# Convolution, mixer, attention and experts in one kernel: fewer dummy matmuls, expert biases in two row groups, last residuals on VectorE, a bank apart for the variance

## The chip, the cores and the metric

The kernel runs on one core of one Trainium2 chip. The metric is device time in microseconds (us). Engines: TensorE (PE, its weight loads PEld), VectorE (DVE), ScalarE (ACT), GpSimd (POOL) and SyncE (SP), which issues the transfers. TensorE writes into PSUM, which has eight banks.

## What is computed

The input x is 8 images of 32 channels and 16 x 16 pixels. Cut to what matters here:

```python
# a 1x1 layer, a depthwise 3x3 convolution, silu, a two-way state-space mixer, batch norm, a gate:
x = gated_mixer(x)                                   # g * x + x
t = tokens(x)                                        # 8 x 256 tokens x 32
t = t + attention(layernorm(t))                      # causal
h = layernorm(t)
p = softmax(h @ router_w + router_b)                 # 8 experts
top_p, top_i = top_k(p, 2); top_p /= top_p.sum(-1)
out = einsum("bnd,edc->bnec", h, expert_w) + expert_b
t = t + sum over the two chosen experts of top_p * out
```

## The kernel before

All of it stays on chip. The 8 images are two halves (bh = 0 and 1) of four images each; a half is a tile of 128 partitions (four images times 32 channels) by 256 pixels. Pixels go in blocks of 128, so there are four output blocks, k = 0 to 3, and blocks 0 and 1 belong to half 0. Each engine has a program written out by hand, and runs it in that order; semaphores join the engines. Nothing is scheduled by a planner.

An fp32 matmul stands in the trace as two pieces, a bf16 one as one. So `x16` at L587 is eight matmuls.

- Start, L571 to L607: `keep_warm(8)`, eight matmuls on a tile of zeros whose result nobody reads (L569, bf16, 512 columns each), then the 1x1 layer (L576) as soon as the pack `pa` and x are loaded; ScalarE copies it out (L352); the folding of weights (L580), four taps of the convolution for each half (L587) while VectorE does the other five (L1066) and adds both (L1073); ScalarE's silu (L361), then its load of another function table (L363) and an exponential (L365). TensorE folds three more weights (L594, L596), runs `keep_warm(5)`, and then the step sizes (L605), which wait for silu. VectorE (L1095, L1097) and ScalarE (L389, L391) turn them into decays, on which all of the mixer rests.
- End of the mixer, L778 to L802: groups 0 to 7 of the state-space scan; `outputs(i)` multiplies a group's matrix with its values (L721) and, for the second group of a unit, adds the carried state (L727). `states` (L709) makes that state, ScalarE copies it (L433). `mean_squares(u)` (L734) feeds the norm on ScalarE (`rms`, L454 and L456). The last group's output goes through VectorE (`gated`, L1156), ScalarE's square (L429), `mean_squares(3)` and the norm before the last `mixer_out` (L792).
- Second norm, router and experts, L1010 to L1033: for each half `centre2` (L915), ScalarE's square (L513), `variance2` (L920), ScalarE's root (L517, L519), VectorE's scaled tile h2 (L1267), the router: first the bias (`route_bias`, L927, one row of contraction), then the weights (`route`, L933), into `router_bank[bh]`, which `variance2` has used before. VectorE's selection of two experts is a chain of some fifteen small instructions (L1277 to L1345). `experts(j)` (L947) is one image's product with all 8 experts, in the 32 rows of the array that hold this image; images 4 to 7 wait until VectorE has weighed images 0 to 3 (`weighted`, L1354, `mix_ready`). `keep_warm` stands at L1012, L1019, L1025 and L1029, the last with 12 matmuls.
- End, L1034 to L1043: for each output block `mixed_head(k)` starts the sum in PSUM with the residual (`t2` times the identity, L968) and adds the expert biases (`wtt`, the turned weights, L971); `mixed(k)` adds the eight weighed products (L982, for the last block four, as VectorE sums the halves, L1408). ScalarE copies each block out (`store_copy`, L536) and SP stores it (L275). `weights_turned(bh)` (L955) and ScalarE's `w_copy` (L531) make `wtt`. Blocks take turns in two banks, `mixed_bank`.

Of the kernel before, what the change touches and what calls it, by code (L numbers as in the profile page):

```python
# [28 lines left out]
ALU = mybir.AluOpType  # L29
ACT = mybir.ActivationFunctionType  # L30
# [44 lines left out]
def program(nc, x_in, pa_in, pb_in, pc_in, pd_in, out):  # L75
    ctx = ExitStack()
    with ctx:
# [163 lines left out]
        wt_bank = [bank[5], bank[5]]  # L241
# [4 lines left out]
        router_bank = [bank[5], bank[0]]  # L246
        mixed_bank = [bank[4], bank[0]]
# [96 lines left out]
        def _(act):  # L344
# [170 lines left out]
            def ln2_root(bh):  # L515
                act.wait_ge(S["var2_done"], bh + 1)
                act.activation(l2[:, bh, :], router_bank[bh][:, 0:L], ACT.Ln, bias=eps[:, :]).then_inc(S["l2_ready"], 1)  # L517
# [16 lines left out]
            def store_copy(k):  # L534
                act.wait_ge(S["mixed"], k + 1)
                act.activation(fin[:, k * Q:(k + 1) * Q], mixed_bank[k % 2][:, 0:Q], ACT.Copy)\  # L536
                   .then_inc(S["fin_ready"], 1)
# [21 lines left out]
            store_copy(2)  # L559
            store_copy(3)  # L560
# [3 lines left out]
        def _(pe):  # L564
# [7 lines left out]
            keep_warm(8, 7)  # L572
# [25 lines left out]
            keep_warm(5, 7)  # L598
# [114 lines left out]
            def outputs(i):  # L713
# [4 lines left out]
                y = [unit[i // 2][C * q:C * q + C, Q * (k % NC):Q * (k % NC) + Q] for q in range(BQ)]  # L718
                for q in range(BQ):
                    m = mmat[:, i, q, :]  # L720
                    mm = pe.matmul(y[q], s1t[:, d, k, q, :], m if d == 0 else back(m), start=False, stop=(step == 0))  # L721
                if step == 1:
                    pe.wait_ge(S["h_copied"], BH * d + bh + 1)
                    pe.wait_ge(S["cpfx_ready"], d + 1)
                    for q in range(BQ):
                        r = slice(C * q, C * q + DI)
                        mm = pe.matmul(y[q], hst[r, d, bh, :], cpfx[r, d, bh, :], start=False, stop=True)  # L727
                mm.then_inc(S["y_done"], 1)

# [49 lines left out]
            skipped(6)  # L779
            outputs(6)  # L780
            skipped(7)
            states(1, 1)
            mean_squares(2)
            outputs(7)
# [132 lines left out]
            def variance2(bh):  # L917

                pe.wait_ge(S["c2sq_ready"], bh + 1)
                pe.matmul(router_bank[bh][:, 0:L], packs["mean32"], c2sq[:, bh, :], start=True, stop=True)\  # L920
# [30 lines left out]
            def weights_turned(bh):  # L951
                pe.wait_ge(S["w_ready"], bh + 1)
                if bh:
                    pe.wait_ge(S["wt_copied"], 1)
# [3 lines left out]
            def mixed_head(k):  # L958

                bh = k // NC  # L960
                o = mixed_bank[k % 2][:, 0:Q]
                pe.wait_ge(S["t2_ready"], bh + 1)
                pe.wait_ge(S["cen2_ready"], 2)
# [565 lines left out]
```

## Time and profile before

| | us |
|---|---|
| median of 3 runs | 93.61 |
| lowest and highest | 93.31, 93.78 |
| the profiled execution | 94.22 |
| its span in the profile | 92.4 |
| around the span | 1.8 |
| TensorE busy | 82.9 |
| VectorE busy | 57.9 |
| ScalarE busy | 40.7 |

The trace is of one execution; starts are counted from the beginning of its span. The chain of waits goes back from the last instruction: at each step to what released it. Its rows give the time by which each step carries the end forward, which for pipelined matmuls is less than what one of them lasts. The timeline gives each group of instructions from its first start to its last end.

### The profile page before, as it was taken

Reading aid. Unit: us, or ns where it says so; the run is one execution under the profiler, and the core shown is the slowest. Engines: PE = TensorE matmul, PEld = TensorE weight load, DVE = VectorE, ACT = ScalarE, POOL = GpSimd, SP = SyncE. Lnnn points to the kernel's source line nnn. Section 1 sums busy time; section 2 is a strip of 40 time slices with the busy share of each in tenths; the row PEclk is TensorE's granted clock in tenths of the full one; section 3 lists DMA queues with packets and bytes.
Section 4 is the critical chain, followed back from the end, with each engine's and each line's share of the span. In section 5 each row is a group of like instructions: output and inputs, shape, how many; then the busy total and the mean of one; then the engine's idle time right before and its main releaser. Section 6 shows DMA issues by size and latency. Waiting matters only on the chain.

```text
span 92.4 us, 1937 instructions
## 1 busy us (share of the span) xinstructions
PE 82.9 (90%) x740; PEld 54.2 (59%) x744; DVE 57.9 (63%) x149; ACT 40.7 (44%) x93; POOL 20.2 (22%) x31
## 2 busy tenths in 40 slices
PE   4999999994999999896589799999999989999890
PEld 1458774553666564445344676767474555789780
DVE  1329968999989999641543359177129789894000
ACT  4031277979739512354379741714660521011011
POOL 6050005967899009800000000000000000000000
DMA  2993000000000000000000000000000000000001
GB/s 32 402 366 146 0 0 0 0 0 0 0 11 0 7 0 0 0 7 0 0 0 4 0 0 7 0 0 0 0 7 0 0 0 0 0 11 28 28 0 57
DMA packets 1305, 2.57 MB, mean 28 GB/s; under 512 B 144, under 2 KB 784, under 8 KB 1296
## 3 DMA queue, kind: packets, MB, share of 16 engines
q1 hardware_dynamic: 1152, 2.31, 6.9%
q10 hardware_dynamic: 144, 0.14, 0.4%
q8 instruction: 6, 0.10, 0.4%
q14 instruction: 3, 0.02, 0.1%
HBM read 2.19 MB, written 0.26 MB: 26 GB/s over the span
## 4 chain that ended last, share of the span: by engine, by line
PE 67%; DVE 15%; ACT 10%; issue 5%; DVEq 0%; ACTq 0%
PE banks L569 8%; PE banks L982 7%; DVE lmat L1135 5%; PE banks L947 4%; PE banks L587 4%; DVE pre L1128 4%; PE banks L669 3%; PE banks L904 3%; PE banks L734 3%; PE banks L686 2%; PE banks L971 2%; PE banks L576 2%; ACT data L503 2%; PE banks L872 2%; PE banks L721 2%
## 5 line engine op out<-in xcount | busy, mean ns | idle before, releaser
L569 PE MATMUL banks<-warm 128*128 128x512 bf16 x40 | 11.8, 429 | 1.4 <-DVE warm L1048 1.2
L1135 DVE TENSOR_TENSOR_SCAN lmat<-banks,data 128x512 f32<-128x512 f32 x8 | 9.8, 1220 | 0.8 <-PE banks L669 0.7
L569 PEld LDWEIGHTS banks<-warm 128*128 128x128 bf16 x44 | 4.4, 108 | 6.1 <-issue 2.0
L982 PE MATMUL banks<-pa,lmat 128*128 128x128 f32 x56 | 6.9, 279 | 0.2 <-issue 0.2
L982 PEld LDWEIGHTS banks<-pa,lmat 128*128 128x128 f32 x56 | 6.6, 192 | 0.3
L297 POOL TENSOR_TENSOR data<-pa,dt_dir 128x512 f32<-128x512 f32 x4 | 4.0, 1039 | 8.7 <-DVE dt_dir L1111 8.7
L1354 DVE TENSOR_TENSOR lmat<-banks,wtok 128x256 f32<-128x256 f32 (+1 forms) x12 | 5.5, 503 | 0.2
L536 ACT ACTIVATE fin<-banks 128x128 f32<-128x128 f32 x4 | 1.1, 278 | 9.9 <-PE banks L982 9.9
L1141 DVE TENSOR_TENSOR mmat<-banks,lmat 128x512 f32<-128x512 f32 x8 | 5.3, 669 | 0.0
L503 ACT ACTIVATE data<-banks 128x384 f32<-128x384 f32 x8 | 3.4, 492 | 3.0 <-PE banks L888 2.9
L297 POOL TENSOR_TENSOR data<-pb,dt_dir 128x512 f32<-128x512 f32 x4 | 4.1, 1042 | 0.0
L947 PE MATMUL banks<-pd,h 32*128 32x256 f32 x32 | 4.1, 399 | 0.0
L686 PE MATMUL banks<-s 16*128 16x128 f32 x64 | 4.0, 321 | 0.0
L454 ACT ACTIVATE yln<-banks,eps 128x256 f32<-128x256 f32 x4 | 1.9, 473 | 4.4 <-PE banks L734 4.4
L1241 DVE TENSOR_REDUCE nmax<-banks 128x2 f32<-128x256 f32 x4 | 1.7, 420 | 3.4 <-PE banks L860 3.4
L669 PE MATMUL banks<-pa,da 128*128 128x128 f32 x16 | 2.5, 278 | 1.5 <-DVE lmat L1135 1.5
L587 PE MATMUL banks<-o1p,diag 128*128 128x256 f32 x16 | 3.7, 385 | 0.0
L624 PE MATMUL banks<-o,fold_w 128*128 128x512 f32 x8 | 3.6, 592 | 0.0
L314 POOL TENSOR_TENSOR pre<-tap,pre 128x510 f32<-128x510 f32 (+2 forms) x3 | 3.4, 1149 | 0.4 <-ACT tap L384 0.2
L686 PEld LDWEIGHTS banks<-s 16*128 16x128 f32 x64 | 2.5, 182 | 1.6 <-issue 1.6
L306 POOL TENSOR_TENSOR wbx<-s1t,lmat 128x128 f32<-128x128 f32 x4 | 2.1, 533 | 5.9 <-DVE lmat L1135 4.4
L721 PE MATMUL banks<-mmat,s1t 128*32 128x128 f32 x64 | 3.4, 285 | 0.0
(200 smaller groups left out, 184.3 us busy)
## 6 DMA issues: line engine op xcount, KB each, us to landing
pc<-in_pc SPq DMA_DIRECT2D x1, 962.5 KB, 7.1
pb<-in_pb SPq DMA_DIRECT2D x1, 446.0 KB, 3.8
pd<-in_pd SPq DMA_DIRECT2D x1, 336.0 KB, 7.5
x<-in_x SPq DMA_DIRECT2D x1, 256.0 KB, 3.0
out<-fin SPq DMA_DIRECT2D x4, 64.0 KB, 1.6
pa<-in_pa ACTq DMA_DIRECT2D x1, 133.5 KB, 3.2
```

The lines of the kernel that those rows point to most:

```text
L297: pool.tensor_tensor(data1[:, i, :, :], one.rearrange("p (o t) -> p o t", o=1).to_broadcast([P, BQ, Q]), spread(dt_dir[:, d, BQ * k:BQ * k ...
L503: act.activation(probt[:, b, :], bank[ST_BANK[b]][:, 0:384], ACT.Exp).then_inc(S["prob_ready"], 1)
L569: pe.matmul(bank[scratch][:, :], warm[:, 0:P], warm[:, :], start=True, stop=True)
L587: mm = pe.matmul(conv_bank[bh][:, 0:L], diag[:, t, :], o1p[:, bh, t // 3:t // 3 + H, t % 3:t % 3 + W], start=(i == 0), stop=(i == len(PE_T ...
L669: mm = pe.transpose(dab_bank[:, Q * q:Q * q + Q], da[:, col:col + 1].to_broadcast([P, P]), packs["ident"] if d == 0 else packs["rev"])
L686: mm = pe.matmul(g_ps[:, q, :], s1[r, d, bh, at], c if d == 0 else back(c), start=True, stop=True)
L721: mm = pe.matmul(y[q], s1t[:, d, k, q, :], m if d == 0 else back(m), start=False, stop=(step == 0))
L947: mm = pe.matmul(e_bank[q][:, 256 * i:256 * i + 256], h2[r, bh, Q * i:Q * i + Q], packs["experts"][r, :], start=True, stop=True)
L982: mm = pe.matmul(o, mix[:, k, e, :, :], packs["ident"], start=False, stop=(e == terms - 1))
L1135: dve.tensor_tensor_scan(lmat[:, i, :], dab_bank, data1[:, i, :, :].rearrange("p q t -> p (q t)"), 0.0, ALU.mult, ALU.add).then_inc(S["sca ...
L1141: dve.tensor_tensor(mmat[:, i, :, :], g_ps, lmat[:, i, :].rearrange("p (q t) -> p q t", q=BQ), ALU.mult)\
L1354: dve.tensor_tensor(mix[:, blks[0]:blks[0] + n, :, q, :], e_bank[q][:, :].rearrange("p (k e c) -> p k e c", k=NC, e=E)[:, c0:c0 + n, :, :] ...
```

## The change

- `keep_warm` at the start has 6 matmuls for 8, the one ahead of the step sizes 2 for 5. Around the second norm the counts go from 2, 2, 4, 12 and 1 to 1, 1, 4, 6 and none, in other banks and behind other waits.
- `variance2` of both halves writes into a bank of its own, `var2_bank`; with this the router's bias needs no longer wait for the root, and stands ahead of the dummies: for half 0 ahead of `variance2(0)` and `attend(1)`.
- In the mixer `states(1, 1)` stands ahead of `outputs(6)`, and `outputs(7)` is split: its products come before `mean_squares(2)`, its carried state after.
- The biases of two blocks are added by two matmuls one after the other, on rows 0 to 31 and 32 to 63 of the array and into two banks (`expert_bias`). They start the sums. Blocks have the banks 4, 0, 3 and 4.
- The residual stays on TensorE for blocks 0 and 1 (`residual_term`); for blocks 2 and 3 VectorE adds it as it copies the block out (`finish`), in place of ScalarE's copies.

```diff
-        wt_bank = [bank[5], bank[5]]
+        wt_bank = [bank[4], bank[5]]
...
-        router_bank = [bank[5], bank[0]]
-        mixed_bank = [bank[4], bank[0]]
+        var2_bank = bank[5]
+        router_bank = [bank[0], bank[3]]
+        mixed_bank = [bank[4], bank[0], bank[3], bank[4]]
...
             store_copy(1)
             w_copy(1)
-            store_copy(2)
-            store_copy(3)
...
-            keep_warm(8, 7)
+            keep_warm(6, 7)
...
-            keep_warm(5, 7)
+            keep_warm(2, 7)
...
             skipped(6)
+            states(1, 1)
             outputs(6)
             skipped(7)
-            states(1, 1)
+            output_terms(7)
             mean_squares(2)
-            outputs(7)
+            output_carry(7)
...
-                pe.wait_ge(S["l2r_ready"], bh + 1)
+                pe.wait_ge(S["o_n_ready"], bh + 1)
...
+            def expert_bias(bh):
+
+                pe.wait_ge(S["wt_copied"], bh + 1)
+                pe.wait_ge(S["gap_ready"], bh + 1)
+                if bh:
+                    pe.wait_ge(S["fin_ready"], 1)
+                for c in range(NC):
+                    r = slice(BQ * E * c, BQ * E * (c + 1))
+                    pe.matmul(mixed_bank[NC * bh + c][:, 0:Q], packs["experts_b"][r, :], wtt[r, bh, :], start=True, stop=False)
+
+            def residual_term(k):
+                pe.matmul(mixed_bank[k][:, 0:Q], packs["ident"], t2[:, 0, Q * k:Q * k + Q], start=False, stop=False)
...
-            pe.wait_ge(S["o_n_ready"], 1)
-            keep_warm(2, 0)
+            route_bias(0)
+            keep_warm(1, 5)
             variance2(0)
             attend(1)
-            route_bias(0)
             route(0)
             experts(0)
             experts(1)
-            keep_warm(2, 0)
+            pe.wait_ge(S["l2_ready"], 1)
+            keep_warm(1, 5)
...
-            pe.wait_ge(S["o_n_ready"], 2)
-            keep_warm(4, 3)
             route_bias(1)
+            pe.wait_ge(S["cen2_ready"], BH)
+            keep_warm(4, 4)
             route(1)
             weights_turned(0)
-            keep_warm(12, 3)
+            pe.wait_ge(S["l2_ready"], BH)
+            keep_warm(6, 5)
             experts(4)
...
-            mixed_head(0)
+            expert_bias(0)
+            residual_term(0)
             mixed(0)
-            mixed_head(1)
+            weights_turned(1)
+            residual_term(1)
             mixed(1)
-            weights_turned(1)
-            mixed_head(2)
-            mixed_head(3)
-            keep_warm(1, 3)
+            expert_bias(1)
             mixed(2)
             mixed(3)
...
+            def finish(k):
+                dve.wait_ge(S["mixed"], k + 1)
+                dve.tensor_tensor(fin[:, k * Q:(k + 1) * Q], mixed_bank[k][:, 0:Q], t2[:, 1, Q * (k - NC):Q * (k - NC) + Q], ALU.add)\
+                   .then_inc(S["fin_ready"], 1)
...
+            dve.wait_ge(S["fin_ready"], NC)
+            finish(2)
+            finish(3)
```

TensorE around the second norm of half 0, before. Names: `t`, `c2sq`, `h` are the tiles of the second norm, `data` and `val` those of attention, `pd` holds router and experts, `ones` is the row that spreads the bias.

```order
L915 MATMUL banks<-t,pc 128x256
L569 MATMUL banks<-warm 128x512 x2
L920 MATMUL banks<-c2sq,pc 128x256
L904 MATMUL banks<-data,val 32x256 x4
L904 MATMUL banks<-data,val 32x128 x4
L904 MATMUL banks<-data,ones_k 32x256 x4
L904 MATMUL banks<-data,ones_k 32x128 x4
L927 MATMUL banks<-pd,ones 128x64
L933 MATMUL banks<-pd,h 128x32 x2
```

The same place in the changed kernel:

```order
L927 MATMUL banks<-t,pc 128x256
L941 MATMUL banks<-pd,ones 128x64
L568 MATMUL banks<-warm 128x512
L934 MATMUL banks<-c2sq,pc 128x256
L916 MATMUL banks<-data,val 32x256 x4
L916 MATMUL banks<-data,val 32x128 x4
L916 MATMUL banks<-data,ones_k 32x256 x4
L916 MATMUL banks<-data,ones_k 32x128 x4
L947 MATMUL banks<-pd,h 128x32 x2
```

The router's bias has moved from behind the attention of half 1 to ahead of the variance.

TensorE at the end, before, from block 1 on (`t` is the residual, `wtt` the turned weights, `lmat` holds the weighed products):

```order
L968 MATMUL banks<-t,pa 128x128
L971 MATMUL banks<-wtt,pd 128x128
L982 MATMUL banks<-pa,lmat 128x128 x8
L955 MATMUL banks<-pa,wtok 64x128
L968 MATMUL banks<-t,pa 128x128
L971 MATMUL banks<-wtt,pd 128x128
L968 MATMUL banks<-t,pa 128x128
L971 MATMUL banks<-wtt,pd 128x128
L569 MATMUL banks<-warm 128x512
L982 MATMUL banks<-pa,lmat 128x128 x12
```

Those of the changed kernel:

```order
L968 MATMUL banks<-pa,wtok 64x128
L982 MATMUL banks<-t,pa 128x128
L993 MATMUL banks<-pa,lmat 128x128 x8
L979 MATMUL banks<-wtt,pd 128x128 x2
L993 MATMUL banks<-pa,lmat 128x128 x12
```

Between block 1's products and the last twelve there stood a turn of weights and five matmuls; now there stand two, on two row groups, and the turn has gone ahead of block 1.

## Rows read from the trace of the kernel before

**Rows 1.** The page's part 4: share of the span by engine

```profile
PE 67%; DVE 15%; ACT 10%; issue 5%; DVEq 0%; ACTq 0%
```

**Rows 2.** The chain of waits, first 13 us: start us, us, what

```profile
1.17 3.60 PE banks L569 x8
...
6.89 3.65 PE banks L587 x16
...
11.40 1.19 PE banks L569 x5
12.58 0.81 PE banks L605 x8
```

**Rows 3.** The timeline, first 14 us: start, us, engine, line, what, idle before

```profile
3.92 0.87 DVE L1052 TENSOR_SCALAR diag<-pa 128x128 f32<-128x128 f32 x4 [2.80 <-DMA pa<-in_pa]
...
10.96 0.91 ACT L361 ACTIVATE o<-convs,pa 128x256 f32<-128x256 f32 x2 [3.76 <-DVE convs L1073]
...
11.89 1.28 ACT L363 ACT_TABLE_LOAD   x1
...
13.19 0.23 ACT L365 ACTIVATE neg_a<-pb 128x32 f32<-128x32 f32 x1
...
13.86 0.23 ACT L389 ACTIVATE dt_exp<-dt_neg 128x32 f32<-128x32 f32 x1 [0.45 <-DVE dt_neg L1097]
```

**Rows 4.** Two lines asked for: ns of one, minimum, median, maximum

```profile
L576 PEld LDWEIGHTS banks<-x,pa x4: 337/337/337, 4.1 to 5.4; 128*128 128x128 f32 x4
...
L580 PEld LDWEIGHTS banks<-pb x2: 181/182/184, 6.4 to 6.5; 32*128 32x128 f32 x2
```

**Rows 5.** Busy us by stretch: PE, PEld, DVE, ACT, POOL, granted clock, DMA

```profile
40.00:50.00 10.00, 7.64 (x45) 4.26 (x46) 4.25 (x15) 6.10 (x13) 0.00 (x0) 1.00 0.00 1
...
70.00:80.00 10.00, 9.58 (x58) 5.38 (x55) 8.71 (x34) 2.25 (x8) 0.00 (x0) 1.00 0.00 0
```

**Rows 6.** The chain of waits at 39 to 40 us

```profile
39.42 0.63 PE banks L734 x2
40.05 0.36 PE banks L721 x8
```

**Rows 7.** The timeline of ScalarE at 40 to 42 us

```profile
40.59 0.42 ACT L456 ACTIVATE yrs<-yln 128x256 f32<-128x256 f32 x1
...
41.28 0.42 ACT L429 ACTIVATE ysq<-yg 128x256 f32<-128x256 f32 x1 [0.27 <-DVE yg L1156]
```

**Rows 8.** The timeline around the first half's logits, 67 to 69 us

```profile
67.81 0.42 DVE L1267 TENSOR_TENSOR h<-cen,l2r 128x256 f32<-128x256 f32 x1 [1.29 <-ACT l2r L519]
68.19 0.29 PEld L927 LDWEIGHTS banks<-pd,ones 1*128 1x128 f32 x2 [0.20 <-issue]
...
68.55 0.52 PEld L933 LDWEIGHTS banks<-pd,h 128*128 128x128 f32 x4
```

**Rows 9.** The timeline of VectorE, last product of the first half

```profile
77.83 0.68 DVE L1354 TENSOR_TENSOR lmat<-banks,wtok 128x512 f32<-128x512 f32 x1
```

**Rows 10.** The chain of waits, last 15 us

```profile
78.01 1.74 PE banks L947 x15
79.75 0.42 PE banks L968 x2
80.17 0.41 PE banks L971 x2
...
82.56 0.22 PE banks L968 x2
...
85.70 0.48 PE banks L971 x2
...
87.02 0.16 issue
87.18 2.85 PE banks L982 x24
```

**Rows 11.** The chain of waits, four row groups side by side

```profile
55.14 0.22 PE banks L860 x8
```

More of the change, by code:

```diff
@@ L516, in ln2_root @@
                 act.wait_ge(S["var2_done"], bh + 1)
-                act.activation(l2[:, bh, :], router_bank[bh][:, 0:L], ACT.Ln, bias=eps[:, :]).then_inc(S["l2_ready"], 1)
+                act.activation(l2[:, bh, :], var2_bank[:, 0:L], ACT.Ln, bias=eps[:, :]).then_inc(S["l2_ready"], 1)
                 act.wait_ge(S["l2_ready"], bh + 1)
@@ L711, in states, with output_of, output_terms @@
                 mm.then_inc(S["h_done"], 1)
-            def outputs(i):
+            def output_of(i, q):
+                k = blk_of(*groups[i])
+                return unit[i // 2][C * q:C * q + C, Q * (k % NC):Q * (k % NC) + Q]
+            def output_terms(i):
                 d, bh, step = groups[i]
@@ L717, in outputs, with output_carry @@
                 pe.wait_ge(S["s1t_copied"], BH * d + bh + 1)
-                y = [unit[i // 2][C * q:C * q + C, Q * (k % NC):Q * (k % NC) + Q] for q in range(BQ)]
                 for q in range(BQ):
                     m = mmat[:, i, q, :]
[L721 to L727, printed above, removed]
+                    mm = pe.matmul(output_of(i, q), s1t[:, d, k, q, :], m if d == 0 else back(m), start=False, stop=(step == 0))
+                if step == 0:
+                    mm.then_inc(S["y_done"], 1)
+            def output_carry(i):
+                d, bh, step = groups[i]
+                pe.wait_ge(S["h_copied"], BH * d + bh + 1)
+                pe.wait_ge(S["cpfx_ready"], d + 1)
+                for q in range(BQ):
+                    r = slice(C * q, C * q + DI)
+                    mm = pe.matmul(output_of(i, q), hst[r, d, bh, :], cpfx[r, d, bh, :], start=False, stop=True)
                 mm.then_inc(S["y_done"], 1)
+            def outputs(i):
+                output_terms(i)
+                if groups[i][2] == 1:
+                    output_carry(i)
             def mean_squares(u):
@@ L919, in variance2 @@
                 pe.wait_ge(S["c2sq_ready"], bh + 1)
-                pe.matmul(router_bank[bh][:, 0:L], packs["mean32"], c2sq[:, bh, :], start=True, stop=True)\
+                if bh:
+                    pe.wait_ge(S["l2_ready"], 1)
+                pe.matmul(var2_bank[:, 0:L], packs["mean32"], c2sq[:, bh, :], start=True, stop=True)\
                   .then_inc(S["var2_done"], 1)
@@ L952, in weights_turned @@
                 pe.wait_ge(S["w_ready"], bh + 1)
[L953 to L954 removed]
+                pe.wait_ge(S["cen2_ready"], BH)
                 pe.transpose(wt_bank[bh][0:NC * BQ * E, 0:Q], wtok[:, bh, :, :], packs["ident"])\
                   .then_inc(S["wt_done"], 1)
[L958 to L963, printed above, removed]
[L964 to L971 removed]
+            def expert_bias(bh):
+                pe.wait_ge(S["wt_copied"], bh + 1)
+                pe.wait_ge(S["gap_ready"], bh + 1)
+                if bh:
+                    pe.wait_ge(S["fin_ready"], 1)
[4 more added lines that the diff above has]
+                pe.matmul(mixed_bank[k][:, 0:Q], packs["ident"], t2[:, 0, Q * k:Q * k + Q], start=False, stop=False)
             def mixed(k):
[L975 removed]
+                o = mixed_bank[k][:, 0:Q]
                 if k == NBLK - 1:
@@ L1018, in _ @@
             experts(1)
-            keep_warm(2, 0)
+            pe.wait_ge(S["l2_ready"], 1)
+            keep_warm(1, 5)
             centre2(1)
```

11 lines of the change are left out of this document (2 added, 9 removed).

## The prediction, made before the changed kernel was run

> **What bounds the kernel now.** I read the page's chain first: TensorE carries 67% of the span, VectorE 15%, ScalarE 10% [rows 1]. So what TensorE does without need on this chain is worth its full length, and elsewhere nothing. Then the chain in order of time, for where dummies and the last blocks stand on it [rows 2, 10], and the timeline at each edit, for what becomes late next. The profiled execution took 94.22 us for a span of 92.4, and the median of the runs is 93.61: the sum below is a difference, taken off either.
>
> **Eight dummies become six.** The eight carry the chain from 1.17 to 4.77 us [rows 2], 0.45 each. The pack `pa` is there at 3.92, when VectorE starts on it [rows 3]; x was asked for at the same time and is the shorter wait. Six dummies end near 3.8, so now `pa` is last. The first layer's weight load started at 4.1 [rows 4]; it can start at about 3.97, and then has no running matmul to hide behind, one load of 0.34 at most. I take 0.37 of the 0.43 that a dummy's time would give; the bounds are 0.2 and 0.45. What hangs on it is ScalarE's copy, VectorE's five taps and silu, all in a row, so the gain reaches silu whole.
>
> **Five become two.** They run from 11.40 to 12.59, and the step sizes L605 follow at 12.58 [rows 2]. Silu ends at 10.96 + 0.91 = 11.87 [rows 3], so L605 waited 0.7 for dummies. Two dummies at 1.19 / 5 = 0.24 end at 11.40 + 0.48, with silu, and L605 could follow it 0.7 sooner. Next late is ScalarE: it loads a table after silu and then computes L365, which ends at 13.19 + 0.23 = 13.42, where L389, next on the chain, started at 13.86 [rows 3]. L389 can follow at 13.44: gain 0.42, not 0.7. Both early edits together: 0.37 + 0.42 = 0.79. The decays, and with them POOL's products and everything behind, move as one; all inputs have landed by then. Bounds 0.2 and 0.85.
>
> **The mixer's end.** All groups of matmuls are the same, in another order. `mean_squares(2)` (0.63) ran ahead of `outputs(7)`'s products (0.36) [rows 6]; these now come first, and the root for unit 2 comes 0.36 later. The last output is ready when it was. But ScalarE's L456 ended at 40.59 + 0.42 = 41.01 and the square of the last output began at 41.28 [rows 7]. L456 now ends at 41.37, and the square, behind it in ScalarE's queue, begins at 41.40: a loss of 0.12. Everything behind it waits for this square. The bounds are -0.1 (a gain, if the earlier state lets the carry start sooner) and 0.4 (the whole shift).
>
> **Router of half 0.** Its bias loads began at 68.19 and the router's own at 68.55 [rows 8]. With the bias gone ahead, the router could start 0.36 sooner, but h2 is ready only at 67.81 + 0.42 = 68.23 [rows 8]. So 68.27: gain 0.28. VectorE's selection, `residual(1)`, `centre2(1)`, `variance2(1)` and the scaled tile of half 1 follow one from the other. Ahead of `variance2(0)` the bias fits: it takes the place of a dummy while TensorE waits for ScalarE's square. Bounds 0 (it delays the variance) and 0.36.
>
> **Twelve dummies become six.** This looks like the largest edit, and I count it at 0.05. The twelve end at 78.01, but the last image's product needs VectorE's fourth `weighed` tile, which ends at 77.83 + 0.68 = 78.51 [rows 9], and the eight experts' matmuls end at 79.75 [rows 10]. That is 1.24 behind the tile, about the four pieces of one image with their loads (0.18 each [rows 4], 0.21 of columns each). VectorE, with the 0.28 from above, is the bound; the dummies only held back images that are not last. Bounds 0 and 0.15.
>
> **Block 0.** Before: residual 0.42, bias 0.41, and sixteen pieces from 80.58 to 82.56, 1.98 [rows 10]. After: the bias pair uses the same row shape as the expert matmuls ahead of it, in other row groups and banks; eight pieces in four row groups add 0.22 [rows 11]. I take 0.2 for the pair. Then the residual at 0.42, for it costs 0.42 behind 32-row work and 0.22 behind full-height work [rows 10]. The products then keep the full height: 16 x 2.85 / 24 = 1.90. So 2.81 becomes 2.52: gain 0.29. Bounds: pair wholly hidden, 0.49; pair in series, 0.62, gain -0.13.
>
> **Block 1.** Before 0.22 + 0.41 + 1.98 = 2.61 [rows 10]. After: the turn of weights, one piece, 0.12, residual 0.22, products 1.90, in all 2.24. Gain 0.37, bounds 0.15 and 0.45. VectorE makes the weights of half 1 while block 0's products run. ScalarE still copies block 1 out before it copies the turned weights, so this wait stays as it is.
>
> **Blocks 2 and 3.** Before: 0.48 + 0.42 (as at 79.75) + 0.41 (as at 80.17) + 0.16 + 2.85 = 4.32 [rows 10]. After: the pair from standstill, 0.48 if two row groups cost what one does, the step to full height between 0.08 (1.98 - 1.90) and 0.20 (0.42 - 0.22), 0.14 taken, and 2.85: 3.47. Gain 0.85; if the pair is in series 0.41 less. VectorE's `finish` does 128 columns from PSUM in place of ScalarE's copy of the same; VectorE took 0.68 for 512 columns, 0.17 per 128 and some fixed time, so I set it equal, with 0.1 either way. It has nothing else to do by then, and the stores are issued as far apart as before.
>
> **Sum.** 0.79 - 0.12 + 0.28 + 0.05 + 0.29 + 0.37 + 0.85 = 2.51. The profiled execution would take 91.7, the median 91.1.
>
> **A rule that speaks against the change.** The first dummies run at the low level: the weight loads of L576 take 337 ns and those of L580, from 6.4 us on, 182 [rows 4], so TensorE went from 1.2 to 2.4 GHz between the two, after dummies and L576 without a pause. The granted clock column says 1.00 everywhere and does not show this. With six dummies there is a pause of some 0.3 us before L576. The Trainium skill (TensorE: Matmul & The Clock Gate, "The HAM clock gate") says that the throttled state is the default and that sustained activity releases it; by that rule the pause could put the rise off. No row here shows a rise with a pause ahead of it. For the later dummies there is one: from 40 to 50 us TensorE was busy for 7.64 of 10 us, with pauses, and stayed at the high level, while from 70 to 80 it was busy for 9.58 [rows 5]; seven dummies less at 0.24 take 1.7 off, to 7.9.
>
> **Rivals.**
> 1. The pairs run in series, or the residual behind them waits longer: 0.42 less at block 0 and 0.41 less at the end, 91.9. For it: L971 alone pays 0.2 above its columns. Against it: rows 11. Chance 0.14.
> 2. The early gain is eaten. The rise of the clock comes later by a microsecond or so, half of that is lost in L587 at the low level, or ScalarE's copy of the first layer starts no sooner: 91.7 to 91.9. Chance 0.13.
> 3. The other side: the pause puts the rise off until after L587. Its sixteen pieces take 3.65 at the high level [rows 2] and would take 7.3. At most 3.65 is added on the way to silu, some tenths less as VectorE's own five taps take nearly as long as L587 does now: 93.61 - 2.51 + 3.4 = 94.5. It decides once TensorE does more than about 2.5 us of that work, plus those tenths, at half rate. Chance 0.05.
> 4. The change removes only what was hidden: TensorE is on the chain at the end, but VectorE or ScalarE takes every place that is freed, as they do for the twelve dummies. What stays is block 2 and 3's 0.4 or so: 93.2. Chance 0.04.
> 5. More than forecast, by the upper bounds of the blocks and of the router: 90.5. Chance 0.12.
>
> **Numbers.** The forecast has the remaining 0.52, with a spread of 90.7 to 91.5 of its own. The range 90.4 to 92.2 leaves out rivals 3 and 4 and the ends of 1, 2 and 5. A measurement tells about 0.5% from no change, 0.47 us; within that fall part of rival 4 and the space between 2 and 3, 0.05 together. Slower is rival 3 and a fall of the clock late in the kernel, 0.06. Faster 0.89.
>
> **What would show it.** L576's matmuls start near 4.1, L580's loads stay at 182 ns, and L389 starts near 13.1. The square of the last output starts 0.12 later than all else implies. The router's loads follow h2 by 0.04. The last expert image ends about 1.2 behind VectorE's fourth tile, with TensorE idle ahead of it. Between block 1's weights copy and the first of the last 24 pieces lie 0.6 us, not 1.5. I would be wrong first where an instruction's doubled time shows the low clock past 7 us, or where the pair's loads are in a row.

## The result, and the profile after

Four executions of the changed kernel took 90.66, 90.73, 94.0 and 101.61 us, beside a median of 93.69 for the kernel before on the same chip (93.31 to 94.19). The ratio is 0.9677 (95% interval 0.9598 to 0.9757), faster: 90.7 us on this chip, 90.6 taken off the 93.61 of the prediction, where the forecast was 91.1 with a range of 90.4 to 92.2. Ratios, here and below, leave out executions over 1.5% above the fastest of their kernel, so that the 94.0 and the 101.61 are not in it; the median of all four is 92.37. What those two are, and whether the change makes them, is the first subject of the experiments. In the 101.61 the profile shows TensorE's clock at its lower level; the 94.0 was not profiled, and a later execution of the same time was. The terms of the sum are read from traces, stage by stage, where the clock is at its high level.

The execution that was profiled is the one of 101.61 us. Its busy times and its slices (lines of the page: engine, busy us, share of the span; then forty slices of 2.5 us, in tenths):

```profile
PE 89.8 (90%) x723; PEld 57.3 (57%) x726; DVE 59.3 (59%) x151; ACT 40.0 (40%) x91; POOL 20.2 (20%) x31
...
PE   5899999939999999999985697999999998999790
...
PEclk9999999995555555555599999999999999999999
```

TensorE is busier than before, 89.8 us for 82.9, although it has less to do: from 22.5 to 50 us it ran at half its rate. The windows of the same execution (stretch, length, busy us and count of each engine, granted clock, share of transfers) place the fall:

```profile
20.50:22.50 2.00, 0.25 (x8) 0.06 (x4) 2.00 (x3) 1.75 (x3) 1.71 (x2) 1.00 0.00 0
22.50:24.00 1.50, 1.50 (x12) 0.82 (x12) 1.30 (x3) 1.42 (x3) 1.17 (x1) 0.55 0.00 0
24.00:28.00 4.00, 4.00 (x44) 3.19 (x40) 2.01 (x3) 1.47 (x4) 3.83 (x6) 0.50 0.01 4
```

A granted clock of 0.50 is the lower of the two levels, 1.2 GHz. It came behind a stretch in which TensorE did 0.25 us of work in 2 us, waiting for VectorE's scan (a pause of 1.75 us, up to 22.50). The rest of this trace is at the high level and shows the change itself. The chain from the last expert images on (start, us carried, engine and line; it answers to [rows 10]; L979 are the biases, L982 the residual, L993 the weighed products, L1420 VectorE's `finish`):

```profile
87.37 1.18 PE banks L961 x5
88.55 0.06 PE banks L979 x2
...
88.68 0.04 PE banks L979
88.71 0.48 PE banks L961 x2
89.19 0.42 PE banks L982 x2
89.61 1.79 PE banks L993 x16
91.40 0.11 PE banks L968
91.51 0.22 PE banks L982 x2
91.73 1.80 PE banks L993 x16
...
94.04 0.49 PE banks L979 x4
94.53 2.89 PE banks L993 x24
97.44 0.29 DVE fin L1420
```

What the reader is to see: the first bias pair stands in the midst of the last expert image and carries the chain by 0.10 in all; the second pair, from standstill, takes 0.49, what one bias alone took before (0.48 [rows 10]); the residual has left the last stretch.

The start of the same execution, in the timeline (start, length, engine, line, operation, count, idle time before and what ended it; it answers to [rows 3]):

```profile
4.25 1.76 PE L575 MATMUL banks<-x,pa 128*128 128x256 f32 x4 [0.34 <-DMA pa<-in_pa]
...
6.36 3.72 PE L586 MATMUL banks<-o1p,diag 128*128 128x256 f32 x16
...
10.51 0.91 ACT L362 ACTIVATE o<-convs,pa 128x256 f32<-128x256 f32 x2 [3.77 <-DVE convs L1084]
...
12.74 0.23 ACT L366 ACTIVATE neg_a<-pb 128x32 f32<-128x32 f32 x1
12.87 0.22 ACT L390 ACTIVATE dt_exp<-dt_neg 128x32 f32<-128x32 f32 x1
```

TensorE now stands still for 0.34 us until `pa` is there, and the exponential starts at 12.87 for 13.86. The experiments show that not all of this 0.99 is the change's.

### The profile page after: what moved, and what is told of

Read it like the earlier page. It is cut to its first block, busy times and chain, and to the rows that moved or that the text cites. A ratio compares the mean times of both kernels' runs of the same rounds, so it can differ in the third digit from the quotient of the medians.

```text
span 99.8 us, 1903 instructions
## 1 busy us (share of the span) xinstructions
PE 89.8 (90%) x723; PEld 57.3 (57%) x726; DVE 59.3 (59%) x151; ACT 40.0 (40%) x91; POOL 20.2 (20%) x31
## 4 chain that ended last, share of the span: by engine, by line
PE 59%; DVE 17%; ACT 12%; issue 4%; DMA 3%; ACTq 0%; DVEq 0%
PE banks L993 6%; PE banks L668 6%; PE banks L685 5%; PE banks L655 5%; PE banks L723 5%; PE banks L745 4%; DMA pa<-in_pa 3%; DVE pre L1139 3%; PE banks L916 3%; DVE conv L1077 3%; PE banks L961 3%; DVE lmat L1146 2%; PE banks L733 2%; ACT data L504 2%; PE banks L884 2%
## 5 line engine op out<-in xcount | busy, mean ns | idle before, releaser
L568 PE MATMUL banks<-warm 128*128 128x512 bf16 x27 | 8.4, 435 | 1.3 <-DVE warm L1059 1.2
L993 PE MATMUL banks<-pa,lmat 128*128 128x128 f32 x56 | 6.8, 277 | 0.0
L993 PEld LDWEIGHTS banks<-pa,lmat 128*128 128x128 f32 x56 | 6.5, 192 | 0.1
L685 PE MATMUL banks<-s 16*128 16x128 f32 x64 | 6.2, 475 | 0.0
L568 PEld LDWEIGHTS banks<-warm 128*128 128x128 bf16 x30 | 2.9, 109 | 4.2 <-issue 1.4
L723 PE MATMUL banks<-mmat,s1t 128*32 128x128 f32 x64 | 5.2, 420 | 0.0
L1167 DVE TENSOR_TENSOR yg<-banks,s 128x256 f32<-128x256 f32 x4 | 1.7, 425 | 5.9 <-PE banks L733 5.9
L655 PE MATMUL banks<-s,skip_w 32*32 32x128 f32 x64 | 5.2, 416 | 0.0
L668 PE MATMUL banks<-pa,da 128*128 128x128 f32 x16 | 3.3, 346 | 1.8 <-DVE lmat L1146 1.8
L504 ACT ACTIVATE data<-banks 128x384 f32<-128x384 f32 x8 | 3.4, 493 | 3.0 <-PE banks L900 2.9
L745 PE MATMUL banks<-ysq,pc 128*128 128x256 f32 x8 | 4.2, 624 | 0.4 <-ACT ysq L430 0.4
L668 PE MATMUL banks<-pb,da 128*128 128x128 f32 x16 | 4.5, 435 | 0.0
L961 PEld LDWEIGHTS banks<-pd,h 32*128 32x128 f32 x32 | 3.4, 184 | 1.5 <-issue 1.3
L430 ACT ACTIVATE ysq<-yg 128x256 f32<-128x256 f32 x4 | 1.7, 417 | 6.5 <-DVE yg L1167 6.5
```

The source lines that it names most:

```text
L568: pe.matmul(bank[scratch][:, :], warm[:, 0:P], warm[:, :], start=True, stop=True)
L655: pe.matmul(unit[u][r, at], skip_w[r, d, r], s1[r, d, bh, at], start=True, stop=False)
L668: mm = pe.transpose(dab_bank[:, Q * q:Q * q + Q], da[:, col:col + 1].to_broadcast([P, P]), packs["ident"] if d == 0 else packs["rev"])
L685: mm = pe.matmul(g_ps[:, q, :], s1[r, d, bh, at], c if d == 0 else back(c), start=True, stop=True)
L723: mm = pe.matmul(output_of(i, q), s1t[:, d, k, q, :], m if d == 0 else back(m), start=False, stop=(step == 0))
L745: pe.matmul(yms[u], packs["mean16"], ysq[:, d, bh, :], start=True, stop=True)\
```

## Experiments: the clock

Two faults will be told apart. In the first, the late rise, the clock comes up from its lower level at the start some microseconds late. In the second, the fall, it goes down again behind a pause further on. Theory: what the changed kernel loses against 90.7 comes from the two early edits alone, by these two, and the late edits are sound. Rival: the late edits, with less work on TensorE from 70 to 80 us, cost the clock; or the 94 is disturbance that has to do with no part of the kernel. Each run below is six executions, with the kernel before on the same chip.

### The changed kernel again

No edit.

> The changed kernel as it is, again. Its four executions so far took 90.7, 90.7, 94.0 and 101.6 us; in the profiled one TensorE's granted clock stood at 0.50 from 22.7 to 47 us, behind a pause of TensorE from 20.7 to 22.5. Theory (the change brings the lower clock closer): again one to three of the executions are above 92.5, the others near 90.7. Rival (a chance of the chip, any kernel): none or one above 92.5, and the kernel before shows such executions as often.

Measured: 94.0, 93.81, 90.9, 90.54, 90.77, 94.3; ratio 0.964 (0.9583 to 0.9698). The granted clock is 1.00 in all six. The profiled execution is one of 94.0, and its timeline has the fault near the start:

```profile
4.41 2.07 PE L575 MATMUL banks<-x,pa 128*128 128x256 f32 x4 [0.49 <-DMA pa<-in_pa]
...
6.41 0.80 PE L579 MATMUL banks<-pb 32*128 32x130 f32 x2
...
7.14 6.25 PE L586 MATMUL banks<-o1p,diag 128*128 128x256 f32 x16
...
16.06 0.23 ACT L390 ACTIVATE dt_exp<-dt_neg 128x32 f32<-128x32 f32 x1
```

The weight loads of the taps (the convolution, L586) say why. By line, engine PEld, with their mean in ns, of this execution and then of the one profiled above:

```profile
L586 PEld LDWEIGHTS banks<-o1p,diag 128*128 128x128 f32 x16 | 4.8, 306 | 1.3 <-issue 0.2
```

```profile
L586 PEld LDWEIGHTS banks<-o1p,diag 128*128 128x128 f32 x16 | 2.9, 189 | 0.5
```

TensorE stays at 1.2 GHz through most of the taps, which last 6.25 us for 3.72, and the exponential starts at 16.06, 3.2 us later. Its last load at 337 ns starts at 11.99 and the first at 190 at 12.36. This is the prediction's rival 3, near the price it was given (94.5), but in three executions of six. The granted clock column does not show it.

### The two early edits alone, in the kernel before

```diff
-            keep_warm(8, 7)
+            keep_warm(6, 7)
...
-            keep_warm(5, 7)
+            keep_warm(2, 7)
```

> The kernel before with 6 dummies for 8 and 2 for 5 at the start, nothing else. If the early edit gains what the prediction said (0.79), 92.9; by the changed kernel's trace, where the first exponential of the step sizes starts 0.99 sooner, 92.7. If the fewer early dummies are what makes the clock fall, some executions are above 95; if not, none.

Measured: 96.25, 104.66, 95.35, 98.31, 98.34, 92.97; median 97.28, where the kernel before had 94.34. Granted clocks: 0.962, 0.851, 1.0, 0.982, 0.982, 1.0. So the early edits bring the slow executions, with nothing late changed: five of six are above 95, and one of eleven of the kernel before (104.12). The one undisturbed execution, 92.97, is 1.4 below before's median and 0.4 below its lowest, too little to measure a gain by. In the profiled one the clock fell behind the same pause:

```profile
20.50:22.50 2.00, 0.25 (x9) 0.08 (x2) 2.00 (x3) 1.75 (x3) 1.63 (x2) 0.97 0.00 0
22.50:24.00 1.50, 1.50 (x12) 0.83 (x12) 1.21 (x3) 1.33 (x3) 1.25 (x1) 0.50 0.00 0
```

In the two executions of 98.3 the granted clock of 0.982 means some 3.5 us at the lower level, which costs 1.7 at most, and they are 5.3 above 92.97: an estimate from these numbers, by which they had the late rise too. The rival that blames the late edits falls.

### The change without its early edits

```diff
-            keep_warm(6, 7)
+            keep_warm(8, 7)
...
-            keep_warm(2, 7)
+            keep_warm(5, 7)
```

> The changed kernel with the 8 and 5 dummies of before at the start, the rest as changed. Prediction's own terms: 93.7 - 1.72 = 92.0; by the late stages of the changed kernel's trace (0.25 + 0.60 + 0.53 + 0.92) 91.4. If the fewer early dummies make the clock fall, no execution is slow; if it is the pause at 21 us whatever stands ahead of it, some are.

Measured: 90.6, 91.89, 90.63, 91.78, 91.54, 92.08; median 91.66, ratio 0.9699 (0.9636 to 0.9762). Neither fault shows in six executions. The late edits and the mixer's end carry the change.

What else this trace shows bears on the early edits. It has the 8 and 5 dummies of before, and its taps start sooner than in any other:

```profile
5.62 3.72 PE L586 MATMUL banks<-o1p,diag 128*128 128x256 f32 x16
```

Before they started at 6.82 (on the chain at 6.89 [rows 2]). The loads of the first layer take 187 to 190 ns here and took 337 before [rows 4]: in this execution the clock had risen by 4.14 us. From the taps on, the exponential starts 7.04 us later and the third group's decays (L668, before L669) 16.49 later, to the hundredth as before. So one and the same set of early dummies puts the decays at 23.31 in one execution and at 22.11 in another. That 1.2 us is the moment of the rise, and it is more than the early edits were to gain.

### Work in the pause

Six dummies are put into the pause between the first group's products and its decays, held until ScalarE's `raw` is there, so that they do not run early.

```diff
             products(0)
+            pe.wait_ge(S["raw_ready"], 2)
+            keep_warm(6, 1)
             decays(2)
```

> The changed kernel with six dummies of 512 columns in TensorE's pause between the first products and the third decays (about 1.3 of its 1.75 us). If this pause is what takes the clock down, no execution is above 92 and the fast ones take 90.7. If the pause has no part in it, the executions scatter as those of the changed kernel.

Measured: 90.87, 90.99, 90.37, 91.0, 90.28, 94.09; median 90.93, ratio 0.9637 (0.9587 to 0.9686). The filler leaves 0.35 us of pause in place of 1.75, and the decays start no later (22.41 for 22.50). TensorE's timeline:

```profile
20.59 1.47 PE L568 MATMUL banks<-warm 128*128 128x512 bf16 x6
22.41 0.65 PE L668 MATMUL banks<-pa,da 128*128 128x128 f32 x4 [0.35 <-DVE lmat L1148]
```

No fall of the granted clock; the 94.09, at a granted clock of 1.0, looks like the late rise, which this edit does not touch, but no trace shows it.

### Eight first dummies and the filler

The second five stay two. The kernel is the base of all that follows.

```diff
-            keep_warm(6, 7)
+            keep_warm(8, 7)
...
             products(0)
+            pe.wait_ge(S["raw_ready"], 2)
+            keep_warm(6, 1)
             decays(2)
```

> The changed kernel with both guards of the clock: 8 dummies at the very start again, 2 (not 5) ahead of the step sizes, and six dummies in TensorE's pause at 21 us. If the two slow kinds of execution come from the pause ahead of the first layer (94.0) and from the pause at 21 us (101.6), none of six executions is above 92.2, and the median is 90.4 to 91.2, better than every kernel so far. If they are chance, one in three is above 93.

Measured: 90.9, 91.05, 90.55, 91.31, 90.99, 91.16; median 91.02, ratio 0.970 (0.9653 to 0.9747), and nothing above 91.4. The first layer starts at 4.65 behind the eight dummies and `pa`, and yet the taps start at 6.20, sooner than in the changed kernel (6.36): in this execution the clock rises during the first layer instead of after it. That is not the dummies' doing, as the table below shows: with eight of them the taps start anywhere from 5.62 to 7.11.

### Which dummies guard against what

Eight first dummies, two second ones, no filler:

```diff
-            keep_warm(6, 7)
+            keep_warm(8, 7)
```

> The changed kernel with 8 dummies at the very start for its 6, and nothing else altered. Theory (the pause ahead of the first layer puts the rise of the clock off): no execution near 94; rare ones above 95 from the pause at 21 us may stay. Median 90.6 to 91.5. Rival (it is the two for five ahead of the step sizes, or chance): executions near 94 as before.

Measured: 95.65, 101.75, 102.5, 91.04, 102.49, 101.77; median 101.76; granted clocks 0.945, 0.863, 0.847, 1.0, 0.847, 0.863. Five of six fell, and in the profiled one the clock fell behind a pause of 1.46 us (TensorE's timeline, then two of the windows):

```profile
22.96 0.65 PE L668 MATMUL banks<-pa,da 128*128 128x128 f32 x4 [1.46 <-DVE lmat L1146]
```

```profile
24.00:28.00 4.00, 4.00 (x44) 3.12 (x48) 2.35 (x3) 1.95 (x5) 3.83 (x5) 0.51 0.00 0
28.00:34.00 6.00, 6.00 (x66) 3.68 (x60) 3.44 (x6) 1.90 (x3) 1.62 (x3) 0.50 0.01 4
```

It did not fall in the pause but 1.1 us after its end, by the windows at about 24.1, with TensorE at work again. The first eight guard against the late rise and not against the fall. Then six first ones, five second ones:

```diff
-            keep_warm(2, 7)
+            keep_warm(5, 7)
```

> The changed kernel with 5 dummies for 2 ahead of the step sizes, still 6 at the very start. Theory: executions near 94 stay, one to three of six; the fast ones are at 90.7 + 0.4 = 91.1 if the prediction's 0.42 for the five is right, at 90.7 if silu and ScalarE's table load set the time anyway. Rival: no execution near 94.

Measured: 93.47, 94.34, 90.68, 95.11, 91.38, 90.83, all at a granted clock of 1.0; median 92.42, ratio 0.9696 (0.9629 to 0.9764). In the profiled one the taps took 5.27 us, with the clock up at about 10.1. So five second dummies don't guard the rise. But none of the six fell.

The starts in all traces, in us. The rise is read from the first fp32 weight load of under 200 ns; in the two rows with 4.14 and 4.20 that is the first such load at all, so that the clock rose earlier still:

| kernel | first, second dummies | first fast load | taps | exponential | third decays |
|---|---|---|---|---|---|
| before | 8, 5 | 6.40 | 6.82 | 13.86 | 23.31 |
| early dummies restored | 8, 5 | 4.14 | 5.62 | 12.66 | 22.11 |
| base | 8, 2 | 5.05 | 6.20 | 12.83 | 22.44 |
| eight and two, no filler | 8, 2 | 7.11 | 7.11 | 13.51 | 22.96 |
| base with twelve | 8, 2 | 5.46 | 6.40 | 12.99 | 22.60 |
| base, old mixer order | 8, 2 | 6.58 | 7.00 | 13.51 | 23.14 |
| base, router's bias late | 8, 2 | 4.93 | 6.09 | 12.62 | 22.23 |
| base, residuals on TensorE | 8, 2 | 4.20 | 5.71 | 12.35 | 21.96 |
| base, biases apart | 8, 2 | 6.08 | 6.50 | 13.01 | 22.64 |
| change | 6, 2 | 5.94 | 6.36 | 12.87 | 22.50 |
| early edits alone | 6, 2 | 5.33 | 6.28 | 12.81 | 22.42 |
| change with filler | 6, 2 | 5.30 | 6.24 | 12.80 | 22.41 |
| change, again | 6, 2 | 12.36 | 7.14 | 16.06 | 25.51 |
| six and five | 6, 5 | 10.34 | 6.96 | 15.55 | 24.99 |

With eight first dummies the taps start from 5.62 to 7.11, 6.38 in the mean of nine traces; with six and no late rise at 6.24 to 6.36. The two dummies taken away gain nothing that these starts can show. What the second dummies cost can be read: from the taps to the decays it is 16.49 with five (both traces) and 16.14 to 16.25 with two (nine of the ten traces without a late rise; one had 15.85), 0.35 less.

All executions counted together, those that are some 3 us above their kernel's best at a granted clock of 1.0 (late rise) and those below 0.99 (fall, whatever else they had):

| | late rise | fall |
|---|---|---|
| six first dummies (the change twice, and three variants) | 9 of 28 | |
| eight, in eight variants | 0 of 48 | |
| no filler: change | | 1 of 10 |
| no filler: 6 and 2 in the kernel before; 8 and 2 | | 4 of 6; 5 of 6 |
| no filler: 8 and 5; 6 and 5 | | 0 of 6; 0 of 6 |
| no filler: kernel before | | 3 of 37 |
| with filler, in seven kernels | | 1 of 42 |

The late rise is thereby shown to come from the two dummies taken away, by its undoing. That it is the pause they leave (0.3 to 0.5 us ahead of the first layer) and not their missing work is argued: no run has the one without the other. The length of the pause doesn't decide it. Pauses of 0.34, 0.40 and 0.48 stood ahead of a rise by 5.9, and pauses of 0.31 and 0.49 ahead of one past 10.

For the fall it is shown that work in the pause prevents it, all but once in 42; on one and the same chip the counts are 5 of 6 without the filler and 0 of 12 with it. The second dummies matter too, some 10 us ahead of the pause: without filler 10 of 22 executions fell with two of them, and 3 of 49 with five. How they do it is open. One rival is the pause itself, which was 1.75 in the two traces of falling kernels with two dummies and an early exponential, and 1.46 in the third that fell and 1.45 to 1.46 in four that did not. What decides in which execution the pause takes the clock down stays open.

## Experiments: the terms of the sum

These start from the base above, with both guards, because their differences are smaller than what the clock does. Times of six executions tell about 0.3 us apart on one chip; the smaller terms are read from the traces. The last four ran on another chip than the base, where the kernel before had 93.97 for 94.08.

### Twelve dummies again

```diff
-            keep_warm(6, 5)
+            keep_warm(12, 5)
```

> The kernel of e5 with 12 dummies for 6 ahead of the last four images' experts. Prediction's term: 0.05 slower than e5 (0 to 0.15), as these images wait for VectorE. Rival: the dummies are on the way, six at 0.24 make it 0.5 to 1.4 slower.

Measured: 91.05, 91.58, 90.58, 90.61, 90.67, 91.42; median 90.86 against 91.02 for the base; ratio to before 0.9699 (0.9645 to 0.9753). In the base VectorE's fourth `weighed` tile ends at 76.57 + 0.68 = 77.25 and the experts at 78.49, 1.24 behind; with twelve it ends at 76.73 + 0.68 = 77.41 and they end at 78.65, again 1.24 behind. The dummies that were taken away were on the chain of the kernel before, right ahead of [rows 10], and cost nothing:

```profile
75.42 2.59 PE banks L569 x12
```

### The old order at the mixer's end

```diff
-            states(1, 1)
             outputs(6)
             skipped(7)
-            output_terms(7)
+            states(1, 1)
             mean_squares(2)
-            output_carry(7)
+            outputs(7)
```

> The kernel of e5 with the mixer's end in the old order (states behind the skip of group 7, outputs of group 7 in one piece behind the mean of squares). Prediction: the new order costs 0.12, so this is 0.12 faster than e5. By the trace of e3, where the way from the carried state of unit 2 to the last mean of squares takes 4.31 us against 4.44 in the kernel before, the new order gains 0.13, so this is 0.13 slower.

Measured: 91.75, 90.64, 90.79, 91.25, 90.95, 91.63; median 91.1, ratio 0.9703 (0.9651 to 0.9755): the time can't tell. The chains can. Old order (L733 adds the carried state, L708 is `states`, L723 the products, L745 `mean_squares`):

```profile
37.14 0.42 PE banks L733 x8
...
39.06 0.20 PE banks L708 x8
...
39.88 0.36 PE banks L723 x8
...
41.12 0.42 ACT ysq L430
...
41.59 0.71 PE banks L745 x2
```

New order (the change without its early edits):

```profile
36.12 0.42 PE banks L733 x8
...
37.33 0.20 PE banks L708 x8
37.52 0.22 PE banks L723 x8
...
39.63 0.42 ACT yrs L457
40.04 0.34 ACT ysq L430
...
40.43 0.71 PE banks L745 x2
```

From L733 of unit 2 to the last `mean_squares` the old order takes 4.45 us and the new one 4.31. A gain of 0.14, where the prediction had a loss of 0.12. The kernel before has 4.44 (37.31 to 41.75).

### The router's bias behind the attention again

```diff
-            route_bias(0)
             keep_warm(1, 5)
             variance2(0)
             attend(1)
+            route_bias(0)
             route(0)
```

> The kernel of e5 with the router's bias of half 0 behind the attention of half 1 again, right ahead of the router. Prediction: 0.28 slower than e5, all the way to the end, since h2 then no longer sets the router's start. Rival: VectorE or the attention sets it and the difference is under 0.1.

Measured: 90.97, 91.1, 93.61, 90.95, 90.83, 91.69; median 91.03, ratio 0.9697 (0.9646 to 0.9747), where the times don't resolve 0.3. The 93.61 has a granted clock of 0.961: the one fall with a filler, of unknown cause. In the traces, from the start of ScalarE's last attention exponentials (L504) to the end of `fin` it is 24.15 us (62.94 to 87.09) and in the base 23.88 (63.15 to 87.03): 0.27. The two lines of this kernel's chain, where L943 is the bias and L949 the router; in the base 0.04 of issue and L949 with 0.65 stand there:

```profile
67.05 0.36 PE banks L943 x2
67.41 0.57 PE banks L949 x4
```

### The last residuals on TensorE again

TensorE adds t2 times the identity for blocks 2 and 3 behind the bias pair, and VectorE's last step is a copy.

```diff
             expert_bias(1)
+            residual_late(2)
+            residual_late(3)
             mixed(2)
...
-                dve.tensor_tensor(fin[:, k * Q:(k + 1) * Q], mixed_bank[k][:, 0:Q], t2[:, 1, Q * (k - NC):Q * (k - NC) + Q], ALU.add)
+                dve.tensor_copy(fin[:, k * Q:(k + 1) * Q], mixed_bank[k][:, 0:Q])
```

> The kernel of e5 with the residuals of blocks 2 and 3 on TensorE, behind the bias pair, and VectorE only copying these blocks out. Prediction's prices: two full-height matmuls more, 0.22 each, the change of height is paid once in either kernel: 0.44 slower than e5. If VectorE's sum costs more than a copy, less than that.

Measured: 90.9, 91.29, 91.72, 91.57, 91.71, 91.8; median 91.64, 0.6 above the base; ratio 0.9738 (0.9691 to 0.9785). The chain, of this kernel and of the base:

```profile
82.88 0.49 PE banks L981 x4
83.37 0.64 PE banks L985 x4
84.01 2.69 PE banks L999 x24
```

```profile
83.34 0.49 PE banks L981 x4
83.83 2.89 PE banks L995 x24
```

0.64 is added, and 0.20 of it is the step to the full height, which the products no longer pay: 0.44. And VectorE's last step carries 0.29 as an add (97.44 in the chain above) and 0.29 as a copy.

### Each bias alone

```diff
-            expert_bias(0)
+            expert_bias(0, 0)
             residual_term(0)
             mixed(0)
+            expert_bias(0, 1)
...
-            expert_bias(1)
+            expert_bias(1, 0)
             mixed(2)
+            expert_bias(1, 1)
             mixed(3)
```

> The kernel of e5 with each block's bias on its own: block 1's behind block 0's products, block 3's behind block 2's, so no two biases share the array, and the height changes twice more. If a pair costs what one does (prediction, and 0.49 for the pair in the changed kernel's trace): two times 0.41 to 0.5 more, 0.8 to 1.0 slower than e5. If a pair costs twice one, only the changes of height are added: 0.2 to 0.4.

Measured: 92.25, 92.15, 91.66, 91.99, 91.77, 92.05; median 92.02, 1.0 above the base; ratio 0.9783 (0.9736 to 0.983). Its chain at the end:

```profile
84.09 0.48 PE banks L981 x2
...
86.56 0.41 PE banks L981 x2
86.97 1.10 PE banks L995 x8
```

A bias alone carries 0.48 from standstill and the pair 0.49: two row groups cost what one does. A bias among full-height products adds 0.41 and lengthens what stands behind it, as the 24 products are 1.98 + 1.10 = 3.08 in two parts and 2.89 in one: 0.60 together. The pair saves one such trip per half.

## Why the prediction was right, and where not

By stages, from before's chain [rows 10] and the chain of the base, each as a gain in us:

| term | forecast | measured | from |
|---|---|---|---|
| early, both | 0.79 | some 0.55, of which 0.35 are the second dummies | 91.29 against 90.74 on one chip; 16.49 against 16.14 |
| mixer's end | -0.12 | 0.14 | 4.45 against 4.31 |
| router | 0.28 | 0.27 | 24.15 against 23.88 |
| twelve dummies | 0.05 | 0.0 | 1.24 behind the tile both times |
| block 0 | 0.29 | 0.60 | 79.75 to 82.56, now 78.49 to 80.70 |
| block 1 | 0.37 | 0.53 | 2.66 against 2.13 |
| blocks 2 and 3 | 0.85 | 0.92 | 4.81 against 3.89 |

The first row needs a word. Between the two profiled executions the exponential moved by 0.99 and the decays by 0.81 (23.31 to 22.50). Of this 0.46 is where the taps started (6.82 and 6.36), which the moment of the rise moves by more than that when nothing is edited. The row therefore goes by times, as an estimate: the executions of the change again that had no late rise have a mean of 90.74, and those of the kernel with the early dummies restored, without the 92.08, 91.29 (with it 91.42, and the row would be 0.7).

The measured sum is 3.0, where 2.5 was forecast, and the median times say the same, 93.69 and 90.7. (The spans of the profiled executions, 92.4 and 89.1, differ by 3.3, because before's had a rise as late as 6.40.) The verdict and the range were right. The late terms came to 2.46 for 1.72, 0.74 more, and the early ones to some 0.25 less than forecast, so that the total is nearer than its parts. From the third decays to the end of the span it is 69.1 us before and 66.7 in the kernel with the early dummies restored and in the base: 2.4, which is the late terms once more. The case that came is rival 5 (90.5) by its size, though not by its reasons: the blocks went beyond their upper bounds and the router did not reach its own. Besides it rival 3 came, in one execution of three.

- **Eight become six.** The number fits the profiled execution, by luck: L575 started at 4.25 for 4.56 and silu ended 0.45 earlier, for 0.37. The prediction took `pa`'s landing for what sets the taps' start. But that landing, taken as 3.92 from the one row in [rows 3], is 3.9 to 4.75 in the traces of the 13 kernels, eight dummies end at 4.77 or, where the clock rises early, at 4.36, and the first layer lasts from 1.03 to 2.08 us as the clock rises before, in or behind it. The rise sets the start of the taps, and over nine traces with eight dummies and three with six that start is the same within 0.1. What is left of the term by the times is some 0.2 (0.55 less 0.35), which the scatter does not tell from nothing. The price is the pause. The step that failed is the chance: "The pause puts the rise off until after L587" was given 0.05 as the time of the kernel, because no row showed a rise with a pause ahead of it, and it happens in 9 of 28 executions. The Trainium skill (TensorE: Matmul & The Clock Gate, "The HAM clock gate"), cited in the prediction, has the throttled state as the default, which sustained activity releases. The traces agree in that the first loads take 337 ns where the rise has not come yet, and a rise past 10 us came only with the pause, in two traces, and in 9 of 28 executions by their times; the three other traces with a pause had risen by 5.94. The rule spoke against the change and was weighed too lightly.
- **Five become two.** Its 0.42 was 0.53 at the exponential (7.04 behind the taps with five, 6.51 with two). L389's wait for all of L365 was a wrong reading: the exponential started 0.13 behind it, not 0.23. Of this 0.18 is given back on the way to the decays: they start 9.63 us behind the exponential for 9.45. Three of VectorE's taps (L1139) take 2.98 us there for 2.79, beside POOL's products; that POOL slows them is argued from the trace and not tested.
- **The fall.** The prediction had it as "a fall of the clock late in the kernel", from the dummies taken out at 70 to 80 us. It did not come there in any of the traces. It came from 22.4 to 24.1, in or behind a pause of 1.46 to 1.75 us. A pause of 1.46 was there before, and I had not listed it. The step that failed is the search: I looked at the two stretches where the change takes dummies off [rows 5], not at the longest pause near the beginning.
- **The mixer's end.** Its sign was wrong. The root for the unit before did come later, 3.51 behind L733 (39.63) for 3.29 in the old order (40.43), 0.22 where 0.36 was forecast. The step that failed is "The last output is ready when it was". The earlier `states` lets L708 and the terms L723 of group 6 carry 0.42 (0.20 + 0.22) for 0.56 (0.20 + 0.36), and VectorE starts on the last output 3.38 behind L733 (39.50) for 3.52 (40.66). The timeline has the square 0.04 behind that output's end in both, in the new order at 39.96 and so even before the root's end: the queue cost nothing. (The chain names the root as what released it, and puts it at 40.04.) The gain of 0.14 went a little beyond the far bound (0.1), for the reason that stood there.
- **Router, twelve dummies.** As forecast. The experts end 1.24 behind the fourth tile in all.
- **Block 0.** Two terms mis-sized. The pair, taken at 0.2, is hidden wholly: it carries 0.10 on the chain, but the experts end 1.24 behind the tile, with it in their midst as without. And the products behind full-height work take 1.79 for 1.90: the 2.85 for 24 from which 1.90 was worked out is 2.69 where a residual stands ahead (the last experiment but one), and 16 x 2.69 / 24 = 1.79.
- **Block 1.** The turn carries 0.11 for 0.12, the residual 0.22 as taken, the products 1.80 for 1.90; the same rate. Before, the block took 2.66 from end to end, where the terms gave 2.61.
- **Blocks 2 and 3.** The pair takes 0.49 for 0.48, and step and products together 2.89 for 0.14 + 2.85 = 2.99. The wait ahead of the pair, left as it is in the forecast, is 0.51 for 0.48.
- **Rival 1** (pairs in series) is excluded by the last experiment. **Rival 2** (a rise later by a microsecond or so) did not show with six dummies in five traces: the first fast load was at 5.3 to 5.9, or at 10.3 and 12.4. A scatter of that size is there with eight. **Rival 4** falls with the table.

The kernel to keep is the base, the change with eight first dummies and the filler: median 91.02, and no execution of its six above 91.4, against 92.37 for the change and up to 101.61. The same with twelve late dummies (90.86) is as good within the noise. Its gain over the kernel before is that of the late edits, of the second dummies and of the guards; the first two dummies are back in it.

## What to carry to other kernels

Dummies ahead of the first real matmul are priced not by their own length on the chain but by what stands behind a pause without them: ask what TensorE's loads would take if the clock had not risen, and keep the dummies until the input that is latest in the slowest execution. Where the clock's rise sets a start, one trace on each side measures the rise and not the edit: compare from the first stretch at full rate on, and take the rest from many executions. List every pause like the 1.5 us here that stands behind the rise, also those that the change does not touch, and see that something runs in it. Small matmuls in another row shape belong together, two row groups at once and next to work of the same shape; one that stands alone among full-height ones costs 0.4 us here, and 0.6 with what it adds to its neighbours.

## What was not expected of the hardware

- The rise scatters. With eight dummies that start at 1.17 in every trace, the first fast load is found from 4.14 to 7.11 us (nine traces), and what follows keeps its distances to a few hundredths.
- The late rise: with six dummies and a pause of 0.3 to 0.5 us before the first layer, the rise was past 10 us in two traces (10.3 and 12.4), and 9 of 28 executions are late by their times, while the granted clock column says 1.00. It shows only in durations: loads of 337 for 181 to 191 ns.
- The fall: in one trace the granted clock went to 0.50 at about 24.1, behind a pause of 1.46 us, and stayed there until 34 us, while TensorE was busy for all of the 10 us between; in the profiled execution of the change it stayed for 27 us. Matmuls kept it busy, and yet it did not rise.
- A pair of matmuls on two row groups takes 0.49 where one takes 0.48, and a pair behind an expert image, which has the same row shape, 0.1.
